# Extra TensorE products whose results nobody reads, ahead of TensorE's waits, and another order of the routing steps

## The chip, the cores and the metric

The kernel runs on one core of a Trainium2 chip. The metric is the device time of one execution in microseconds (us). Five engines work side by side, each through its own instruction queue in program order: PE (TensorE, matrix products; PEld is its weight load), DVE (VectorE), ACT (ScalarE), POOL (GpSimd) and SP (SyncE, which here only starts transfers). They wait for each other through semaphores.

## What is computed

Three blocks with residuals on `x` of 1024 tokens by 512, in float32:

```
x = x + cross_attention(layernorm(x), ctx_768)        # 257 keys of 384 per group of 32 tokens, one head
x = x + self_attention(layernorm(x))                  # 16 heads of 32, rotary, groups of 32 tokens
x = x + experts(layernorm(x))                         # 8 experts, the best 2 of each token

def experts(xf):
    scores = sigmoid(xf @ gate_w.T + balance_bias)    # (tokens, 8)
    top, idx = top_k(scores, 2); top = top / (top.sum() + 1e-6)
    out = sum over the two experts e of a token: top_e * (silu(xf @ w1[e].T) @ w2[e].T)
```

## The kernel before

The 1024 tokens are 8 tiles of 128, worked on in 4 pairs (`PAIRS`). The program of every engine is written out by hand, and its text is the order of its work. There is no scheduler. Matrix products are done in float16 parts (high and low) or in float32, which takes the array several passes.

**Cross attention**, then **self attention** run over the four pairs. In `attend(pair)` PE forms the attention outputs of two tiles (L615), then their output projection: 8 products with the high part (L633) and 4 with the low part (L637) for each tile. ACT and DVE copy and round between them. DVE adds the result to `x` and takes its statistics (`last_stats`, L1464 and L1467), POOL takes the inverse root (L1757), DVE scales (`last_scale`, L1140). PE transposes the scaled rows (`features_T`, L372), ACT copies them (L944) and PE forms the gate's `logits` (L653, products with only 8 columns).

**Routing** is done in three portions, `ROUTED`: tiles 0 to 3, 4 and 5, 6 and 7. For each one DVE ranks the experts (`choose_rank`), PE counts how many tokens chose each expert before this one (`choices_before`, L604), DVE turns counts into places (`place`), marks with one-hot matrices which tokens come first (`mark`, L1567 and L1569), and works out gates (`choose_gates`, L1542 to L1545) and row numbers (`slots_out`, L1575 to L1577). With the row numbers POOL writes every token twice into `routed_rows` in DRAM, sorted by expert: 16 indirect transfers (`scatter`, L1820), two for each tile.

**Experts.** The sorted rows are taken 128 at a time. The first two such tiles need no trip through DRAM: PE gathers their rows by products with the one-hot matrices (`no_rows`, L707, and `first_rows`, L718), ACT copies them into `xgT`. Expert weights come in four pieces; ACT makes each one's high part (`cut_high`, L963) and DVE its low part (`cut_low`, L1614). `first_tile_product` (L751) is the first product of the first tile, then a loop handles the others: `hidden_T` (transposes, L372), `first_product` (L769), `second_product` (L787). ACT's silu is L1065, DVE rounds the hidden rows in `cut_hidden` (L1708 and L1710). POOL adds each finished tile to the output with an indirect transfer (L1856).

What sets the order around the change: PE's text from L628 to L795, DVE's text from L1625 to L1670 and its tail `cut_low(expert0, (1,))`, `tiles_of_experts`, `cut_hidden(0)`, `map_of_tiles`, `cut_low(expert0, (2, 3))`, and the text of ACT behind `features_high(PAIRS - 2)`. Before the change `first_tile_product` begins with two waits:

```
pe.wait_ge(s["rt_slots"], len(ROUTED))
pe.wait_ge(s["xgT0"], 1)
```

`rt_slots` is counted up by the last instruction of each `slots_out`, `xgT0` by ACT's copy of the gathered rows.

## Time and profile before

| | us |
|---|---|
| median of 3 runs (lowest, highest) | 537.12 (536.85, 538.25) |
| the profiled execution's own time | 536.98 |
| its span, first to last instruction | 534.4 |
| PE busy | 490.4 (92% of the span) |
| DVE busy | 374.6 (70%) |
| ACT busy | 254.2 (48%) |
| POOL busy | 111.3 (21%) |
| mean granted share of TensorE's clock | 0.963 |

The share of the clock is given by stretch: 1.00 is 2.4 GHz, 0.50 is 1.2 GHz. The page of the profile cuts the span into 40 slices of 13.4 us; in tenths of busy time and of granted clock they read:

```profile
PE   5998889999999999976879899999999999999994
PEclk9898999999999999986869999999999999999997
```

From the 23rd slice on the expert loop takes over; the slices with gaps in PE's row and a low clock ahead of it (numbers 18 to 22 of the row, 227 to 294 us) are the last pair of self attention, the routing and the first expert tile.

### The profile page before, as it was taken

To read this page: it belongs to the slowest core of one execution; us is meant where nothing else is said; L and a number is where in the kernel's file an instruction comes from. 1 tells how busy PE (TensorE), PEld (TensorE's weight loads), DVE (VectorE), ACT (ScalarE), POOL (GpSimd) and SP (SyncE) were. 2 spreads that over 40 slices of the span, in tenths; PEclk is the share of its full clock that TensorE was granted. 3 is DMA by queue.
4 is the path that set the end of the run, shared out by engine and by line. 5 is a ranking of instruction groups with operands and counts; after the bars stand their busy time and mean duration, and the time that the engine had idled before them with its cause. 6 is when DMAs were issued, how large, how long until landed. Compare 5 with 4: busy or idle time off the path is not lost.

```text
span 534.4 us, 11347 instructions
## 1 busy us (share of the span) xinstructions
PE 490.4 (92%) x3746; PEld 286.0 (54%) x3747; DVE 374.6 (70%) x849; ACT 254.2 (48%) x396; POOL 111.3 (21%) x86
## 2 busy tenths in 40 slices
PE   5998889999999999976879899999999999999994
PEld 2753546555675776735565444445444454444443
DVE  5778898777859998888787886763746637673230
ACT  1313555643359293846732745544625446552230
POOL 1032212012160322200663022111121111121112
PEclk9898999999999999986869999999999999999997
DMA  8999697900009996256842589894885947843333
GB/s 309 405 397 380 242 389 262 371 3 1 1 1 381 379 383 219 72 212 229 288 189 100 154 270 260 270 257 129 230 243 141 258 112 218 238 82 73 59 59 40
DMA packets 55201, 110.95 MB, mean 208 GB/s; under 512 B 24416, under 2 KB 25600, under 8 KB 50048
## 3 DMA queue, kind: packets, MB, share of 16 engines
q1 hardware_dynamic: 25296, 87.80, 45.4%
q10 hardware_dynamic: 25568, 12.94, 10.1%
q0 software_dynamic: 4304, 9.77, 8.6%
q8 instruction: 21, 0.34, 0.3%
q14 instruction: 12, 0.10, 0.1%
HBM read 75.82 MB, written 29.43 MB: 197 GB/s over the span
## 4 chain that ended last, share of the span: by engine, by line
PE 52%; DVE 27%; issue 6%; DMA 5%; ACT 4%; POOL 3%; SPq 2%; DVEq 1%; ACTq 0%; POOLq 0%
PE bank L787 18%; PE bank L769 17%; DMA ctx_region<-in_ctx 4%; PE bank L372 3%; PE bank L540 3%; PE bank L556 3%; DVE wbuf L1614 2%; DVE small L1164 2%; POOL small L1757 2%; DVE small L1161 2%; DVE small L1131 1%; PE bank L751 1%; DVE ctx_region L1411 1%; PE bank L633 1%; DVE ctx_region L1413 1%
## 5 line engine op out<-in xcount | busy, mean ns | idle before, releaser
L769 PE MATMUL bank<-wbuf,ctx_region 128*128 x480 | 106.9, 379 | 0.0
L1614 DVE SCALAR_TENSOR_TENSOR wbuf<-ctx_region,wbuf 128x2048 f32 (+1 forms) x28 | 62.9, 2288 | 29.4 <-ACT wbuf L963 28.0
L1856 POOL DMA_INDIRECT out<-misc,ints x21 | 39.8, 1894 | 203.0 <-ACT misc L1046 144.4
L769 PEld LDWEIGHTS bank<-wbuf,ctx_region 128*128 128x128 f16 x480 | 46.1, 98 | 51.9
L963 ACT ACTIVATE wbuf<-ctx_region 128x2048 f32 (+1 forms) x28 | 52.0, 1902 | 27.6 <-issue 17.2
L1757 POOL TENSOR_TENSOR small<-small 128x2 f32<-128x2 f32 (+2 forms) x25 | 27.4, 1098 | 162.9 <-DVE small L1137 160.1
L1065 ACT ACTIVATE ctxT_region<-bank 128x512 f32<-128x512 f32 x42 | 25.0, 597 | 67.0 <-PE bank L769 56.0
L787 PE MATMUL bank<-wbuf,xn 128*128 x240 | 53.4, 379 | 0.9 <-DVE xn L1714 0.9
L787 PE MATMUL bank<-wbuf,actT 128*128 x240 | 53.4, 379 | 0.0
L787 PEld LDWEIGHTS bank<-wbuf,xn 128*128 128x128 f16 x240 | 23.5, 98 | 29.4 <-issue 1.7
L1708 DVE CAST ctxT_region<-ctxT_region 128x1024 f16<-128x1024 f32 x21 | 14.6, 694 | 34.9 <-ACT ctxT_region L1065 34.9
L787 PEld LDWEIGHTS bank<-wbuf,actT 128*128 128x128 f16 x240 | 23.5, 98 | 28.3
L1710 DVE TENSOR_TENSOR ctxT_region<-ctxT_region 128x1024 f16<-128x1024 f32 x21 | 25.7, 1226 | 0.7
L372 PE MATMUL bank<-ident,ctxT_region 128*128 128x128 f16 x336 | 22.4, 219 | 3.1 <-DVE ctxT_region L1708 1.3
L372 PEld LDWEIGHTS bank<-ident,ctxT_region 128*128 128x128 f16 x336 | 20.4, 98 | 8.4 <-DVE ctxT_region L1708 1.8
L1820 POOL DMA_INDIRECT routed_rows<-shared,ints x16 | 19.1, 1194 | 21.6 <-DVE ints L1577 15.8
L556 PE MATMUL bank<-ctx_region,wbuf 128*128 128x256 f16 x192 | 21.6, 273 | 0.7 <-DVE ctx_region L1288 0.7
L556 PE MATMUL bank<-shared,wbuf 128*128 128x256 f16 x192 | 21.6, 273 | 0.0
L1070 ACT COPY actT<-bank 128x1024 f16<-128x1024 f16 x11 | 11.0, 1001 | 21.9 <-PE bank L372 20.1
L556 PEld LDWEIGHTS bank<-ctx_region,wbuf 128*128 128x128 f16 x192 | 18.7, 98 | 3.5 <-DVE ctx_region L1288 0.9
L1004 ACT ACTIVATE ctxT_region<-ctxT_region 128x512 f32<-128x512 f32 x8 | 5.0, 630 | 32.4 <-DVE ctxT_region L1445 32.4
L986 ACT COPY ctxT_region<-misc 32x512 f32<-32x512 f32 x32 | 19.7, 615 | 1.1 <-DVE misc L1456 0.8
(232 smaller groups left out, 858.9 us busy)
## 6 DMA issues: line engine op xcount, KB each, us to landing
ctx_region<-in_experts SPq DMA_DIRECT2D x28, 1024.0 KB
routed_rows<-ctxT_region SPq DMA_DIRECT2D x1, 16900.0 KB, 50.8
ctxT_region<-in_ctxT SPq DMA_DIRECT2D x8, 1542.0 KB, 11.1
ctx_region<-in_ctx SPq DMA_DIRECT2D x8, 1536.0 KB, 8.9
ctx_region<-routed_rows ACTq DMA_DIRECT2D x21, 260.0 KB, 3.2
wbuf<-in_experts SPq DMA_DIRECT2D x4, 1024.0 KB
out<-x ACTq DMA_DIRECT2D x8, 256.0 KB
wbuf<-in_wqT SPq DMA_DIRECT2D x4, 256.0 KB, 5.3
```

Source lines behind the costliest of these rows:

```text
L372: last = nc.tensor.transpose(dst[0:piece.shape[1], at:at + n], piece, identity[0:n, 0:n])
L556: mm = nc.tensor.matmul(bank[first + e // 2][:, e % 2 * 256:e % 2 * 256 + 256], w[w_part][:, k, e * P:(e + 1) * P], xnT_homes[pair % 2][:, ...
L769: mm = nc.tensor.matmul(bank[half][:, :], xgT[:, b, x_part, k * P:(k + 1) * P], w16[:, ds(at + (w_part + k * EH + half * 512), 512)], star ...
L787: mm = nc.tensor.matmul(bank[5 + b][:, :], hT[b][:, h_part, k * P:(k + 1) * P], w16[:, ds(at + (w_part + W2_AT + k * D), D)], start=(k == ...
L963: nc.scalar.activation(w16[:, ds(at + (HIGH + n * PIECE), PIECE)], src_[:, n * PIECE:(n + 1) * PIECE], ACT.Copy, scale=W_SCALE).then_inc(s ...
L986: op = nc.scalar.copy(p_T[part, t, :, b * L:(b + 1) * L], soft_T[part, t, :].rearrange("p (h l) -> p h l", l=L))
L1065: nc.scalar.activation(h[:, half * 512:half * 512 + 512], bank[half][:, :], ACT.Silu, scale=1.0 / W_SCALE).then_inc(s["h"], 1)
L1614: nc.vector.scalar_tensor_tensor(w16[:, ds(at + (LOW + n * PIECE), PIECE)], src_[:, piece], W_SCALE, w16[:, ds(at + (HIGH + n * PIECE), PI ...
L1710: tt(h16[:, 1, :], h, h16[:, 0, :], ALU.subtract).then_inc(s["h_lo"], 1)
L1757: nc.gpsimd.tensor_tensor(out_, in_, neg_half[0:parts, 0:n], ALU.pow).then_inc(s[f"{name}_rstd"], 1)
L1820: nc.gpsimd.indirect_dma_start(xs_dram, bass.IndirectOffsetOnAxis(slot_i[:, choice, tile:tile + 1].bitcast(U32), axis=0), xf[:, tile, :], ...
L1856: nc.gpsimd.indirect_dma_start(out, bass.IndirectOffsetOnAxis(idx[:, slot_no:slot_no + 1].bitcast(U32), axis=0), y_out[:, slot_no, :], Non ...
```

## The change

1. PE gets a function `unread(b, count)`: `count` products of a 128x128 identity in float16 with itself repeated to 512 columns, written to PSUM bank `b`, where nothing reads them. A new semaphore `ident16_set` tells PE that the identity is there. It is called at nine places, in the order of PE's work with 6, 8, 5, 9, 3, 3, 5, 8 and 4 products (51 in all).
2. The last pair marks tiles 0 and 1 where it marked tiles 0 to 3, and tiles 2 and 3 behind the statistics. PE gathers tiles 2 and 3 behind `features_T(PAIRS - 1)`.
3. `choose_gates(1)` and `slots_out(1)` move behind the marking of the third portion; `cut_low(expert0, (0,))` moves behind `slots_out(2)`.
4. PE gathers tiles 6 and 7 part by part: the high parts of both, then the low parts.
5. `first_tile_product` no longer waits for `rt_slots`; its two halves are now inside the loop over `k`.
6. ACT's `cut_high` of the fourth piece moves behind its copy of the gathered rows.
7. POOL issues 2 of its transfers ahead of the last inverse root, where it issued 3.

```diff
+            def unread(b, count):
+                pe.wait_ge(s["ident16_set"], 1)
+                for _ in range(count):
+                    nc.tensor.matmul(bank[b][:, :], ident16[:, :], ident16[:, None, :].to_broadcast([P, 4, P]), start=True, stop=True,
+                                     skip_group_check=True)
...
                         join_biases()
+                        unread(4, 6)
                         pe.wait_ge(s["sc_nb"], 2)
...
                     pe.wait_ge(s["z"], 2 * pair)
+                if pair + 2 == PAIRS:
+                    unread(0, 8)
+                if pair + 1 == PAIRS:
+                    unread(4, 3)
...
                     scores(pair)
+                    unread(2, 5)
                     features_T(pair - 1)
+                    unread(2, 9)
                     logits(pair - 1)
+                    unread(2, 3)
...
-            first_rows(0, range(0, ROUTED[0][1]))
+            first_rows(0, range(0, 2))
+            unread(6, 5)
             features_T(PAIRS - 1)
+            first_rows(0, range(2, ROUTED[0][1]))
             pe.wait_ge(s["z"], TILES - 2)
             logits(PAIRS - 1)
             first_rows(0, range(*ROUTED[1]))
+            unread(6, 8)
             choices_before(2)
             no_rows(1)
             first_rows(1, range(0, 2))
-            first_rows(0, range(*ROUTED[2]))
+            for part in range(2):
+                first_rows(0, range(*ROUTED[2]), (part,))
...
-                pe.wait_ge(s["rt_slots"], len(ROUTED))
                 pe.wait_ge(s["xgT0"], 1)
...
+            unread(4, 4)
             first_tile_product()
...
-            cut_high(expert0, 2 * EXPERT, (3,), 0)
...
             first_rows_out(0, s["xgT0"], 1)
+            cut_high(expert0, 2 * EXPERT, (3,), 0)
...
-                        mark(0)
+                        mark_at(0)
+                        mark(range(0, 2))
                 norm_mean(stats, mv, ve, s["ln4_ve"], 2)
+                if pair + 1 == PAIRS:
+                    mark(range(2, ROUTED[0][1]))
...
             choose_scores(1)
-            choose_gates(1)
             logits_out(PAIRS - 1)
             choose_rank(2)
-            slots_out(1)
             last_features_low(0)
             place(2)
-            mark(2)
+            mark_at(2)
+            mark(range(*ROUTED[2]))
             last_features_low(1)
-            cut_low(expert0, 2 * EXPERT, (0,), 0)
+            choose_gates(1)
+            slots_out(1)
             choose_experts(2)
             choose_scores(2)
             choose_gates(2)
             slots_out(2)
+            cut_low(expert0, 2 * EXPERT, (0,), 0)
...
-                    scatter(0, first_to_store[0:2])
+                    scatter(0, first_to_store[0:1])
                     features_low(pair - 1)
-                    scatter(0, first_to_store[2:3])
+                    scatter(0, first_to_store[1:2])
```

PE from the last pair's scores to its output projection, before (L592 scores, L372 transposes, L653 logits, L615 attention outputs, L604 counts, L633 projection):

```order
L592 MATMUL bank<-ctx_region 32x128 x32
L372 MATMUL bank<-consts,misc 128x128 x8
L653 MATMUL bank<-gate_w,ctx_region 128x8 x8
L615 MATMUL bank<-ctxT_region,ctx_region 32x128 x16
L604 MATMUL bank<-ctxT_region,late_consts 128x32
L604 MATMUL bank<-ctxT_region,consts 128x32
L615 MATMUL bank<-ctxT_region,ctx_region 32x128 x16
L633 MATMUL bank<-wbuf,actT 128x512 x8
```

The same place in the changed kernel (its line numbers are 8 to 12 higher; L381 is the unread product):

```order
L600 MATMUL bank<-ctx_region 32x128 x32
L381 MATMUL bank<-ident 128x512 x5
L372 MATMUL bank<-consts,misc 128x128 x8
L381 MATMUL bank<-ident 128x512 x9
L665 MATMUL bank<-gate_w,ctx_region 128x8 x8
L381 MATMUL bank<-ident 128x512 x3
L623 MATMUL bank<-ctxT_region,ctx_region 32x128 x16
L612 MATMUL bank<-ctxT_region,late_consts 128x32
L612 MATMUL bank<-ctxT_region,consts 128x32
L623 MATMUL bank<-ctxT_region,ctx_region 32x128 x16
L381 MATMUL bank<-ident 128x512 x3
L645 MATMUL bank<-wbuf,actT 128x512 x8
```

Four groups of unread products have come in, the last of them where no other instruction stood between the attention outputs and the projection. A little later on PE, from the clearing of the gathered rows (L707) to the last counts (L604), before:

```order
L707 MATMUL bank<-ctxT_region 128x512 x2
L718 MATMUL bank<-misc,shared 128x128 x32
L372 MATMUL bank<-consts,misc 128x128 x8
L653 MATMUL bank<-gate_w,ctx_region 128x8 x8
L718 MATMUL bank<-misc,shared 128x128 x16
L604 MATMUL bank<-ctxT_region,late_consts 128x16
L604 MATMUL bank<-ctxT_region,consts 128x16
```

And in the changed kernel (L722 clears, L733 gathers, L665 logits, L612 counts):

```order
L722 MATMUL bank<-ctxT_region 128x512 x2
L733 MATMUL bank<-misc,shared 128x128 x16
L381 MATMUL bank<-ident 128x512 x5
L372 MATMUL bank<-consts,misc 128x128 x8
L733 MATMUL bank<-misc,shared 128x128 x16
L665 MATMUL bank<-gate_w,ctx_region 128x8 x8
L733 MATMUL bank<-misc,shared 128x128 x16
L381 MATMUL bank<-ident 128x512 x8
L612 MATMUL bank<-ctxT_region,late_consts 128x16
L612 MATMUL bank<-ctxT_region,consts 128x16
```

Half of the gathering now stands behind the transposes, and 8 unread products stand ahead of the counts. DVE behind the marking of the third portion (L1569), before (L1486 low part of the features, L1614 the cut of weight piece 0):

```order
L1569 TENSOR_SCALAR misc<-late_consts,small 128x256 x2
L1486 TENSOR_TENSOR shared<-misc,shared 128x512
L1614 SCALAR_TENSOR_TENSOR wbuf<-wbuf 128x2048
L1522 TENSOR_SCALAR ctxT_region<-ctxT_region 128x16
L1523 TENSOR_SCALAR ctxT_region<-ctxT_region 128x16
```

And in the changed kernel (L1590 marks, L1505 low part, L1561 to L1564 gates of the second portion, L1596 to L1598 its row numbers, L1541 the third portion's experts):

```order
L1590 TENSOR_SCALAR misc<-late_consts,small 128x256 x2
L1505 TENSOR_TENSOR shared<-misc,shared 128x512
L1561 SCALAR_TENSOR_TENSOR ctxT_region<-ctxT_region 128x2
L1563 RECIPROCAL ctxT_region<-ctxT_region 128x2
L1564 SCALAR_TENSOR_TENSOR shared<-ctxT_region 128x2x2
L1596 TENSOR_TENSOR ctxT_region<-ctxT_region,misc 128x2x16
L1597 TENSOR_REDUCE misc<-ctxT_region 128x2x2
L1598 CAST ints<-misc 128x2x2
L1541 TENSOR_SCALAR ctxT_region<-ctxT_region 128x16
```

Six small instructions have taken the place of the cut of piece 0; that cut now stands directly ahead of the cut of piece 1, behind the row numbers of the third portion.

## Rows read from the trace of the kernel before

**Rows 1.** Chain that ended last, in order of time: start us, us, what.

```profile
230.94 2.62 PE bank L633 x8
...
238.06 0.70 DVE x L1464
...
279.70 7.05 PE bank L751 x24
...
317.45 5.18 PE bank L769 x24
```

**Rows 2.** PE's waits from 225 to 312 us: line <- releaser: total, times, longest.

```profile
PE bank L372 <- DVE misc L1140: 3.6, 2, 1.8
PE bank L653 <- ACT ctx_region L944: 3.4, 2, 3.1
PE bank L751 <- DVE ints L1577: 3.1, 1, 3.1
PE bank L633 <- DVE small L1493: 2.8, 1, 2.8
```

**Rows 3.** Stretches: us, busy us (x) of each engine, granted clock third from last.

```profile
242.80:245.50 2.70, 0.00 (x0) 0.00 (x0) 2.63 (x5) 1.46 (x3) 0.00 (x0) 1.00 0.37 100
245.70:255.70 10.00, 9.70 (x88) 7.75 (x89) 8.04 (x29) 7.89 (x19) 0.49 (x1) 0.50 0.64 220
266.20:276.20 10.00, 9.96 (x67) 9.14 (x68) 8.46 (x31) 4.82 (x7) 6.33 (x7) 0.50 0.58 218
279.90:283.00 3.10, 3.10 (x8) 1.06 (x7) 2.96 (x9) 0.00 (x0) 2.27 (x2) 0.50 0.08 30
```

**Rows 4.** Timeline of PE and DVE around 50 us: start, us, instruction [idle before].

```profile
47.20 5.40 PE L445 MATMUL bank<-wbuf 128*128 128x512 f32 x8 [2.29 <-DVE small L1232]
...
53.12 0.68 DVE L1352 SCALAR_TENSOR_TENSOR bo<-rows,bo 32x512 f16<-32x512 f32 x1
53.83 0.42 DVE L1251 TENSOR_TENSOR misc<-bank,small 128x256 f32<-128x256 f32 x1
```

**Rows 5.** Timeline of PE, 219 to 263 us.

```profile
219.18 5.34 PE L582 MATMUL bank<-wbuf,shared 128*128 128x512 f16 x24
224.36 1.85 PE L653 MATMUL bank<-gate_w,ctx_region 128*128 128x8 f32 x16
...
245.83 3.58 PE L653 MATMUL bank<-gate_w,ctx_region 128*128 128x8 f32 x16 [3.08 <-ACT ctx_region L944]
...
252.44 1.94 PE L615 MATMUL bank<-ctxT_region,ctx_region 128*32 128x128 f32 x32
...
261.03 1.95 PE L718 MATMUL bank<-misc,shared 128*128 128x128 f16 x32
```

**Rows 6.** Timeline of DVE, 252 to 298 us.

```profile
252.54 0.77 DVE L1559 TENSOR_TENSOR misc<-bank,misc 128x8 f32<-128x8 f32 x4 [0.98 <-PE bank L604]
...
259.18 0.86 DVE L1567 SCALAR_TENSOR_TENSOR small<-ctxT_region,misc 128x4 f32<-128x4 f32 x1
...
261.31 0.67 DVE L1464 SCALAR_TENSOR_TENSOR x<-bank,x 128x512 f32<-128x512 f32 x1
...
273.93 0.68 DVE L1486 TENSOR_TENSOR shared<-misc,shared 128x512 f16<-128x512 f32 x1
274.54 2.28 DVE L1614 SCALAR_TENSOR_TENSOR wbuf<-wbuf 128x2048 f16<-128x2048 f32 x1
...
287.41 0.69 DVE L1708 CAST ctxT_region<-ctxT_region 128x1024 f16<-128x1024 f32 x1 [3.09 <-ACT ctxT_region L1065]
...
296.08 4.49 DVE L1614 SCALAR_TENSOR_TENSOR wbuf<-ctx_region,wbuf 128x2048 f16<-128x2048 f32 x2
```

**Rows 7.** Timeline of POOL, 272 to 287 us.

```profile
275.75 1.90 POOL L1820 DMA_INDIRECT routed_rows<-shared,ints  x1 [0.31 <-issue]
...
280.43 2.24 POOL L1820 DMA_INDIRECT routed_rows<-shared,ints  x1 [1.51 <-DVE ints L1577]
...
285.75 0.96 POOL L1820 DMA_INDIRECT routed_rows<-shared,ints  x1 [0.30 <-issue]
```

More of the change, by code:

```diff
@@ L85 @@
 qk_ps qkT qb_ps q_bias sc_ps max_step sc_nb sc_exp sc_rinv sc_pm pT_ps pT cv_ps cv_raw cv cvT_ps y_ps x_new
-ptx_zero ln3_ve ln3_rstd ln3_out xnT_ps xnT xnT_lo sw_hi sw_lo sq_ps sk_ps sq sk swapped cosined sined
+ident16_set ptx_zero ln3_ve ln3_rstd ln3_out xnT_ps xnT xnT_lo sw_hi sw_lo sq_ps sk_ps sq sk swapped cosined sined
 rotated k_exp sv_ps sv ss_ps softmax_step s_sub s_exp s_pT p_cols ao_ps ao_hi ao_lo sy_ps x_post x_plus_sbo
@@ L708, in no_rows, with first_rows @@
                                      skip_group_check=True)
-            def first_rows(n, tiles):
+            def first_rows(n, tiles, parts=(0, 1)):
                 for tile in tiles:
                     pe.wait_ge(s["hot"], tile + 1)
-                    pe.wait_ge(s["xf_lo"], tile + 1)
-                    for part in range(2):
+                    for part in parts:
+                        pe.wait_ge((s["xf_hi"], s["xf_lo"])[part], tile + 1)
                         for k in range(KC):
@@ L720, in first_rows @@
                                                   start=False, stop=(tile == TILES - 1), skip_group_check=True)
-                if tile == TILES - 1:
+                if tile == TILES - 1 and 1 in parts:
                     mm.then_inc(s["xgT_ps"], 1)
@@ L734, in _ @@
             first_rows(1, range(0, 2))
-            first_rows(0, range(*ROUTED[2]))
+            for part in range(2):
+                first_rows(0, range(*ROUTED[2]), (part,))
             def first_tile_product():
                 at = 2 * EXPERT
-                pe.wait_ge(s["rt_slots"], len(ROUTED))
                 pe.wait_ge(s["xgT0"], 1)
                 for w_part, x_parts in ((HIGH, (0, 1)), (LOW, (0,))):
-                    for half in range(2):
-                        for k in range(KC):
-                            if w_part == LOW:
-                                pe.wait_ge(s["w1_lo"], k // 2 + 1)
-                            else:
-                                pe.wait_ge(s["w_hi"], k // 2 + 1)
+                    for k in range(KC):
+                        pe.wait_ge(s["w1_lo"] if w_part == LOW else s["w_hi"], k // 2 + 1)
+                        for half in range(2):
                             for x_part in x_parts:
@@ L753, in first_tile_product @@
                                                       stop=(k == KC - 1 and w_part == LOW), skip_group_check=True)
-                        if w_part == LOW:
-                            mm.then_inc(s["h_ps"], 1)
+                            if w_part == LOW and k == KC - 1:
+                                mm.then_inc(s["h_ps"], 1)
             def experts_of(tile):
@@ L1305, in _ @@
                                     ALU.add)
-            nc.vector.tensor_copy(ident16[:, :], ident)
+            nc.vector.tensor_copy(ident16[:, :], ident).then_inc(s["ident16_set"], 1)
             dve.wait_ge(s["cols_in"], 16)
@@ L1560, in place, with mark_at, mark @@
                 then(tt(slot[:, some], bank[within][:, lo * E:hi * E].rearrange("p (t e) -> p t e", e=E), base[:, some, :], ALU.add))
-            def mark(n):
-                lo, hi = ROUTED[n]
-                some = slice(lo, hi)
+            def mark_at(n):
+                some = slice(*ROUTED[n])
                 dve.wait_ge(s["rt_sel"], n + 1)
                 then(nc.vector.scalar_tensor_tensor(hot_at[:, some], sel[:, some, 0], -CHOSEN, slot[:, some, 0], ALU.mult, ALU.add))
-                for tile in range(lo, hi):
+            def mark(tiles):
+                for tile in tiles:
                     ts(hot[:, tile, :], late("places"), hot_at[:, tile:tile + 1], None, ALU.is_equal).then_inc(s["hot"], 1)
@@ L1670, in _ @@
             place(1)
-            mark(1)
+            mark_at(1)
+            mark(range(*ROUTED[1]))
             choose_experts(1)
             choose_scores(1)
-            choose_gates(1)
             logits_out(PAIRS - 1)
             choose_rank(2)
-            slots_out(1)
             last_features_low(0)
             place(2)
-            mark(2)
+            mark_at(2)
+            mark(range(*ROUTED[2]))
             last_features_low(1)
-            cut_low(expert0, 2 * EXPERT, (0,), 0)
+            choose_gates(1)
+            slots_out(1)
             choose_experts(2)
@@ L1843, in _ @@
                     plus_sbo(pair + 2)
-            scatter(0, first_to_store[3:])
+            scatter(0, first_to_store[2:])
             for n in (1, 2):
```

## The prediction

> **What bounds the kernel now.** I read the chain that ended last first. From 317.45 us on it holds PE alone, product after product [rows 1], and no step of the change lies there. So the change is worth what the loop starts earlier. Ahead of it the chain passes between PE and DVE in 228 to 311 us. PE's waits name four gaps there, of 2.8 to 3.6 us in total per line [rows 2]. The stretches then show what follows such gaps: the granted clock is still 1.00 at 242.80 to 245.50, where PE has nothing, and 0.50 (1.2 GHz) in the 10 us behind it, though PE is busy for 9.70 us of them; the same in 266.20 to 276.20 and behind the wait for L751 in 279.90 to 283.00 [rows 3].
>
> At 0.50 the logits (L653) take 3.58 us against 1.85 at 1.00, and 32 records of L615 take 1.94 [rows 5], about half of that (0.98) at 1.00. On 32 gathering products (L718, 1.95 us at 1.00, so 0.98 for 16) it is the same doubling. An unread product has the shape of L582, 24 in 5.34 us [rows 5]: 0.22 us each at 1.00, 0.43 at 0.50.
>
> **Ahead of L445 (6 products).** 6 x 0.22 = 1.3 us in a wait of 2.29 us [rows 4], so it costs nothing. If the clock holds, L445 takes some 3.7 instead of 5.40 us, but DVE comes to L1251, which waits for the transposes behind it, straight from L1352 (53.80 to 53.83) [rows 4]. DVE is full there: 0 gained.
>
> **Pair 2's projection (8 products).** 1.7 us in the wait of 2.8 us [rows 2]. The 24 projection products behind it would take 5.3 us at 1.00 where they took 7 from 230.94 [rows 1]. DVE's choice of experts stands between its two additions, so the second one, L1464 at 238.06 [rows 1], comes when DVE is free: 1.06 earlier. The scores, the softmax and its copies on ACT follow. Lead: 1.06.
>
> **The last pair (5, 9, 3 and 3).** The first 5 and 9 take 1.1 and 1.9 us of waits of about 1.8 and 3.08 us and delay nothing. But will they hold the clock? Behind the 9 there is still about 1.2 us of nothing, then the logits, 3, and 1.2 us more until the softmax's copies come. With the logits as full-time work the clock stayed at 0.50 in 245.70 to 249 [rows 3, 5], so they do not bring it up. I judge it likelier that it falls once more, and take the attention outputs at 0.50. Then the count for DVE's L1559 is there at 251.5 rather than 252.54 (lead 1.04 [rows 6]), the second half ends at 253.45, and the 3 products in front of the projection, which stood in no wait, cost 3 x 0.43 = 1.3 us. The projection's second tile ends near 260.55, where it ended just before 260.4. DVE's second L1464 was held at 261.31 not by PE but by the marks. Two marks fewer (0.65) and L1567, which took 0.86 us beside POOL's subtraction [rows 6] and now comes after it, make DVE free, so PE's 260.6 decides. Lead at the scaled rows: 0.7.
>
> That L1567 waited is what the Trainium skill, "SBUF — State Buffer", section "Who interferes with whom", says of a DVE instruction with two SBUF inputs and a GpSimd one that reads SBUF: one fully blocks for the other. It returns as a rival below.
>
> **Transposes, logits, counts.** The projection has brought the clock up by then, and 5 products and the gathering keep work dense. Transposes 264.05 to 265.1, gathering of tiles 2 and 3 to 266.1 (0.98, moved behind them; ACT's copy needs most of that), logits 1.85 to 267.95. They ended at 269.7, so the lead is 1.75. DVE has its ranks at 269.7. PE gathers tiles 4 and 5 to 268.9 and then stands in 8 unread products until 270.65, 0.95 after the ranks: that is the price of this group. Counts to 271.2, which came at 272.5: lead 1.3. DVE's marks and last low part, L1486 at 273.93 with 0.68 [rows 6], end at 273.2: lead 1.4.
>
> **The reordered tail on DVE.** Before, DVE went on with the cut of piece 0 (2.28), 3 us of small instructions, the cut of piece 1, the tile tables (2.55), and then stood 3.09 us at L1708 for ACT's silu, since PE had stood for the row numbers until 279.70 [rows 1, 2, 6]. Now 1.2 us of gates and row numbers of portion two come first. PE gathers to 274, ACT copies to 275, PE does the 16 high products (3.5 us) meanwhile, and the 8 low ones follow the two cuts, which end at 281.7; the silu is done by 283.7, and DVE comes to L1708 at 284.25 without a wait, 3.15 us before 287.41. The 4 products in front cost nothing, since ACT's copy takes as long. On its own DVE would have the first cut of the loop's weights at 293.0 instead of 296.08 [rows 6].
>
> **POOL.** Row numbers of portion two are now at 274.4 (before: 271.9), so 8 of the 16 transfers stand behind them. Free of cuts one takes 0.96 with 0.30 in front [rows 7], 1.26. Issued during a cut it took 1.90 and 2.24, each ending 0.9 us after that cut did [rows 6, 7]. From 275.3, with cuts in 277.3 to 281.7: 276.3, 278.0, 280.4, 282.6, then 4 x 1.26: 287.65. It ended at 286.71 before, so this queue is later than before by 0.94 and becomes what is late next. ACT waits for its last write (about 1.4 us to land), reads rows, copies the hidden tile, and makes the high part that DVE's cut needs: 6.1 us from POOL's end, 293.75. That is a lead of 2.3 us over 296.08. The first inverse root has one transfer fewer ahead of it, but POOL was free 2 us before it was asked: 0.
>
> **PE in front of the loop.** PE now finishes its second product at about 298 and waits 3 us for the rounded rows, where it waited 1.3. Behind waits of that size the clock fell [rows 2, 3]. Half a fall (3.4 us at 0.50 lose 1.7 in 279.90 to 283.00 [rows 3]) is hidden under DVE's copy, 0.9 us late for PE before. So between 0 and 0.8 us are lost; I take 0.4.
>
> **Sum:** 536.98 - 2.3 + 0.4 = 535.1 for a profiled execution (its span of 534.4 and 2.6 around it). The median of the runs stood 0.14 above that execution: 535.2.
>
> **Costs with two ends.** Each unread product lies between 0.22 and 0.43 us, by the clock it meets. The early group: 0 to 1.3 us if sc_nb came first, which the 2.29 us exclude. The 8 in front of the counts: 0.95 us, or 2.6 at 0.50.  A transfer of POOL during two joined cuts: 1.26 to 4 us; I take the single cut's figures, the nearest rows.
>
> **Rivals.**
>
> 1. *The clock holds through the last pair.* For it: 14 dense products in two waits, and the clock did stay at 1.00 behind the 1.8 us wait at 240. Then the attention outputs end at 252.0, the 3 products cost nothing more than 0.65, the projection ends at 257.85, DVE's L1464 comes at 257.9, logits end at 265.6, counts at 268.8 (8 products overshoot by 0.85), the last low part at 270.6: lead 4.0. The tail adds what it adds above (2.3 less 1.4, 0.9): the first loop cut at 291.2, lead 4.9, less 0.4, plus 0.14: 532.6.
>
> 2. *No change: POOL is shut out by the joined cuts.* A transfer that meets the first cut waits for the second too, ends at 282.6 instead of 280.4, and five follow: 288.9, 1.25 later. With the full 0.8 at the loop: 536.98 - 2.3 + 1.25 + 0.8 + 0.14 = 536.9. Against it: POOL got its turn within 0.9 us of a cut's end both times. For it: nothing stands between the cuts now. By the page of the Trainium skill named above, whichever of the two engines is first holds the pair for its whole instruction, and a cut has two SBUF inputs; if DVE's second cut is first each time, that rule gives this case's time.
>
> 3. *Slower: the 8 products in front of the counts meet a clock of 0.50.* The logits alone kept it there before [rows 3], and gathering tiles 2 and 3 late leaves gaps around the transposes. Logits then end at 270.5, gathering at 272.4, the 8 take 3.46 us instead of 1.73, counts at 276.9, 4.4 us late. As dense work they may bring the clock up halfway, which gives back 1.7. The tail takes 0.9 off: 1.8 to 3.5 late, middle 2.6: 536.98 + 2.6 + 0.14 = 539.7. It turns to a loss once the counts are later than 273.4 (272.5 and the 0.9 that the tail still gives).
>
> **Chances.** Forecast 0.41, rival 1 0.27, rival 2 0.18, rival 3 0.14. What a measurement can tell from no change is about 0.3%, 1.6 us: faster means under 535.5, slower over 538.7. The forecast's own range is 534.0 to 536.3, about 0.65 of it under 535.5. Faster: 0.27 + 0.27 = 0.54; slower 0.14; within 0.32. The range reaches to rival 1 and to the near end of rival 3: 532.2 to 538.2.
>
> **What would show it.** Right: the clock at 1.00 from 228 to about 246, at 0.50 for part of 246 to 256, at 1.00 through 264 to 270; L751's row with two short waits for DVE's cuts in place of one of 3.1 us for row numbers; no wait at DVE's L1708; POOL's 16th transfer ending near 287.7; the loop's first cut near 293.8. Rival 1 shows the clock at 1.00 throughout and that cut near 291. Rival 2 shows a POOL transfer of over 3 us. Rival 3 shows the clock at 0.50 over the 8 products and counts behind 273. I am wrong altogether if the loop's products show gaps behind 320 us that they did not have.

## The result, and the profile after

| | median, us (lowest to highest, runs) | ratio to the kernel before, 95% interval |
|---|---|---|
| first set: the changed kernel | 541.07 (537.71 to 541.84, 6) | 1.0059 [1.0032, 1.0086] |
| the kernel before beside it | 536.99 (535.41 to 538.56, 6) | |
| second set, taken later: the changed kernel again | 536.85 (536.05 to 538.83, 12) | 0.9984 [0.9966, 1.0001] |
| the kernel before beside it | 537.59 (534.41 to 539.55, 32) | |

Slower in the first set, no difference in the second. The forecast was 535.2, likelier faster than not. Neither set bears it out. Two executions far from all others (999.68 us of the kernel before beside the first experiments, 730.26 us of c_order_only) are in no ratio. The rows below are of the profiled execution of the first set: 541.43 us, span 539.5, mean granted clock 0.977 (before: 0.963).

The chain that ended last (start, us, what) answers to [rows 1]. The lines have other numbers in the changed kernel: L645 was L633, L1480 was L1464, L766 was L751 and L784 was L769; L1635 (DVE's cut of expert weights) was L1614 and L1843 (GpSimd's transfers) was L1820. The four rows now read:

```profile
237.69 1.73 PE bank L645 x8
...
242.96 0.70 DVE x L1480
...
309.75 6.78 PE bank L784 x24
...
322.60 5.18 PE bank L784 x24
```

The expert loop's product from which PE works without gaps (the steady product below) stands 5.15 us later than in [rows 1] (322.60 for 317.45), and DVE's second addition already 4.90 later (242.96 for 238.06). So the loss in this execution lies ahead of everything in the tail. The stretches (columns as in [rows 3]) show where the clock now is and is not:

```profile
57.00:63.00 6.00, 6.00 (x32) 1.50 (x25) 5.93 (x14) 1.17 (x5) 0.69 (x1) 0.50 0.49 172
98.00:101.00 3.00, 3.00 (x8) 0.84 (x7) 2.04 (x9) 2.37 (x5) 0.00 (x0) 0.50 0.99 413
247.70:250.40 2.70, 1.88 (x9) 0.68 (x7) 2.63 (x5) 1.46 (x3) 0.00 (x0) 1.00 0.44 112
255.00:258.00 3.00, 3.00 (x48) 2.49 (x42) 2.03 (x10) 2.94 (x8) 0.00 (x0) 0.50 0.80 317
271.10:281.10 10.00, 8.31 (x77) 5.33 (x77) 6.71 (x31) 3.69 (x6) 3.86 (x5) 1.00 0.44 165
306.20:312.60 6.40, 4.91 (x24) 2.70 (x25) 4.61 (x6) 3.93 (x4) 1.62 (x1) 0.50 0.75 239
```

Of the 0.50 stretches of [rows 3] one part is left, 255 to 258; 271 to 281 is at 1.00 throughout. New ones are at 57, 98 and 306. The unread products keep the clock up there: c_order_only below, the same order without them, has it at 0.50 in 233.4 to 236.8, 247.1 to 257.3 and 270.9 to 277.8 us (one trace each). But it didn't pay. The last expected step of the tail is there too. DVE's and GpSimd's timeline around it, to be read against [rows 6, 7]:

```profile
282.37 4.49 DVE L1635 SCALAR_TENSOR_TENSOR wbuf<-wbuf 128x2048 f16<-128x2048 f32 x2
289.25 0.69 DVE L1731 CAST ctxT_region<-ctxT_region 128x1024 f16<-128x1024 f32 x1
300.26 2.29 DVE L1635 SCALAR_TENSOR_TENSOR wbuf<-ctx_region,wbuf 128x2048 f16<-128x2048 f32 x1 [2.26 <-ACT wbuf L979]
```

```profile
274.26 0.96 POOL L1843 DMA_INDIRECT routed_rows<-shared,ints  x1 [0.30 <-issue]
280.45 0.96 POOL L1843 DMA_INDIRECT routed_rows<-shared,ints  x1 [5.23 <-DVE ints L1598]
...
282.98 2.50 POOL L1843 DMA_INDIRECT routed_rows<-shared,ints  x1 [0.30 <-DVE ints L1598]
285.79 1.90 POOL L1843 DMA_INDIRECT routed_rows<-shared,ints  x1 [0.31 <-issue]
...
292.33 0.96 POOL L1843 DMA_INDIRECT routed_rows<-shared,ints  x1 [0.30 <-issue]
```

The two cuts of weight pieces 0 and 1 now follow each other at once, L1731 (L1708 before) has lost its wait of 3.09 us, and the loop's first cut has got one of 2.26: GpSimd sat idle for 5.23 us for the row numbers of the second portion (tiles 4 and 5; portion 1 in the code and below), its last transfer ends at 293.29, and what ACT does for that cut comes behind it. Last, PE's waits from 230 to 317 us, against [rows 2]:

```profile
PE bank L372 <- DVE ctxT_region L1731: 3.5, 1, 3.5
PE bank L381 <- issue: 2.8, 1, 2.8
PE bank L766 <- DVE wbuf L1635: 2.0, 2, 1.2
```

L381 is the unread product. The wait of 2.8 us of pair 2's projection is now charged to it: the product stands behind that wait in PE's program and does not fill it.

### The profile page after: what moved, and what is told of

Its sections match the earlier page's. It is cut to its first block, busy times and chain, and to the rows that moved or that the text cites. A ratio compares the mean times of both kernels' runs of the same rounds, so it can differ in the third digit from the quotient of the medians.

```text
span 539.5 us, 11451 instructions
## 1 busy us (share of the span) xinstructions
PE 495.7 (92%) x3797; PEld 284.1 (53%) x3798; DVE 373.9 (69%) x849; ACT 254.2 (47%) x396; POOL 110.8 (21%) x86
## 4 chain that ended last, share of the span: by engine, by line
PE 59%; DVE 18%; issue 7%; DMA 7%; POOL 4%; ACT 2%; SPq 2%; ACTq 0%; DVEq 0%; POOLq 0%
PE bank L784 19%; PE bank L802 18%; DMA ctx_region<-in_ctx 6%; PE bank L372 4%; PE bank L564 4%; PE bank L548 3%; POOL routed_rows L1843 2%; DVE small L1180 1%; PE bank L529 1%; POOL small L1780 1%; DVE small L1147 1%; DVE small L1177 1%; PE bank L828 1%; PE bank L590 1%; PE bank L645 1%
## 5 line engine op out<-in xcount | busy, mean ns | idle before, releaser
L784 PE MATMUL bank<-wbuf,ctx_region 128*128 x480 | 108.5, 383 | 0.0
L1635 DVE SCALAR_TENSOR_TENSOR wbuf<-ctx_region,wbuf 128x2048 f32 (+1 forms) x28 | 62.9, 2289 | 32.9 <-ACT wbuf L979 31.5
L784 PEld LDWEIGHTS bank<-wbuf,ctx_region 128*128 128x128 f16 x480 | 46.6, 99 | 53.1 <-issue 2.2
L1731 DVE CAST ctxT_region<-ctxT_region 128x1024 f16<-128x1024 f32 x21 | 14.6, 693 | 31.6 <-ACT ctxT_region L1081 31.5
L372 PE MATMUL bank<-ident,ctxT_region 128*128 128x128 f16 x336 | 23.2, 223 | 5.0 <-DVE ctxT_region L1731 3.5
L372 PEld LDWEIGHTS bank<-ident,ctxT_region 128*128 128x128 f16 x336 | 21.0, 100 | 10.4 <-DVE ctxT_region L1731 4.0
L1843 POOL DMA_INDIRECT routed_rows<-shared,ints x16 | 19.0, 1189 | 23.2 <-DVE ints L1598 19.5
```

The lines of the kernel that those rows point to most:

```text
L372: last = nc.tensor.transpose(dst[0:piece.shape[1], at:at + n], piece, identity[0:n, 0:n])
L784: mm = nc.tensor.matmul(bank[half][:, :], xgT[:, b, x_part, k * P:(k + 1) * P], w16[:, ds(at + (w_part + k * EH + half * 512), 512)], star ...
L1635: nc.vector.scalar_tensor_tensor(w16[:, ds(at + (LOW + n * PIECE), PIECE)], src_[:, piece], W_SCALE, w16[:, ds(at + (HIGH + n * PIECE), PI ...
L1843: nc.gpsimd.indirect_dma_start(xs_dram, bass.IndirectOffsetOnAxis(slot_i[:, choice, tile:tile + 1].bitcast(U32), axis=0), xf[:, tile, :], ...
```

## The experiments

All ratios are to the kernel before on the same chip. The traces are compared at fixed instructions: the start in the kernel's trace less the start in the trace before, each less the same shift at 220.65 us (the turning of pair 2's features), so that what happened ahead of the tail is taken out. Negative is earlier. The columns are named by the line and time in the kernel before: L1464, DVE's second addition of pair 2's projection; the last low part of the features (L1486); L1708, DVE's first rounding of hidden rows; DVE's first cut of weights in the expert loop (L1614); PE's steady product (L769). Worked out so:

| kernel | ratio | shift at 220.65 | L1464 at 238.06 | last low part, 273.93 | L1708, 287.41 | first loop cut, 296.08 | steady product, 317.29 |
|---|---|---|---|---|---|---|---|
| changed, first set | 1.0059 | +4.91 | 0.0 | -1.0 | -3.1 | -0.7 | +0.2 |
| changed, second set | 0.9984 | +3.03 | +1.7 | -1.5 | -3.6 | -1.6 | -0.5 |
| a_no_early | 1.0041 | +1.02 | +1.7 | +1.1 | -1.0 | +1.0 | +1.0 |
| b_only_early | 1.0006 | +1.71 | -1.2 | -2.1 | -2.5 | -2.5 | -2.5 |
| c_order_only | 1.0027 | +1.71 | -0.1 | +0.7 | -1.4 | +0.5 | +2.0 |
| d_products_only | 1.0065 | +0.80 | +1.7 | +1.8 | +0.1 | +0.2 | +0.2 |
| e_slots_early | 0.9942 | +2.56 | +1.7 | -1.2 | -4.4 | -4.4 | -3.8 |
| f_ahead_of_wait | 0.9961 | +0.85 | -1.2 | -4.5 | -6.5 | -4.6 | -3.5 |
| g_logits_first | 1.0033 | +4.83 | +1.7 | +1.6 | -0.5 | +1.7 | +2.3 |
| i_both | 0.9955 | +0.84 | -1.2 | -1.6 | -4.8 | -4.8 | -4.8 |
| j_both_hold | 0.9934 | +2.48 | -1.2 | +0.5 | -2.7 | -2.7 | -2.0 |
| k_both_four | 0.9921 | +2.17 | -1.2 | -0.6 | -3.8 | -3.8 | -3.8 |
| l_both_without_three | 0.9950 | +0.40 | -1.2 | -0.1 | -3.3 | -3.3 | -3.3 |
| m_logits_first_none | 1.0020 | +2.84 | -1.3 | +3.6 | +0.6 | +0.7 | +0.7 |
| n_without_early | 0.9958 | +1.23 | -1.2 | -1.5 | -4.7 | -4.7 | -4.7 |
| o_without_unread_tail | 0.9978 | +1.03 | -1.2 | -0.8 | -3.8 | -3.8 | -3.2 |
| p_both_four_again | 0.9971 | +1.10 | -1.2 | +1.4 | -1.8 | -1.8 | -1.8 |

One trace each, while the ratios rest on 6 to 12 runs. The two need not agree: d_products_only's trace is 1.0 us late at the steady product, its ratio says 3.5 us.

### Which half of the change costs

```diff
# a_no_early (the changed kernel without this line)
-                        unread(4, 6)
# b_only_early (the kernel before with this line ahead of L445)
+                        unread(4, 6)
# c_order_only: the changed kernel without any unread(...)
# d_products_only: the kernel before with every unread(...) but the early one
```

> The changed kernel without the six unread products ahead of L453. Theory A (they are the cause): with them the profile of the changed kernel had granted clock 1.00 at 47.6 to 51.0 us and 0.50 at 56.9 to 63.6, where the context products stand in the chain, and pair 2's L623 ended 4.9 us late (233.00 for 228.10). Without them the 0.50 comes back at 47.6 to 51.0, L623 ends near 228.1 to 229, and the time is 541.1 - 4.9 + up to 1 = 536 to 537.5, the same as before. Theory B (the 4.9 us are a chance of landing times, and the loss lies elsewhere, as in the products behind the wait in pair 2's projection): L623 lands anywhere from 228 to 233, and the time stays at 540 to 542.

> The kernel before with only the six unread products ahead of L445. Theory A: clock 1.00 at 47 to 51 us and 0.50 soon after 56 us; pair 2's L615 ends 3 to 5 us later than 228.1, and the time is 537.0 + 3 to 5 = 540 to 542, a loss as large as the whole change's. Theory B: no difference beyond 0.3%, 535.5 to 538.5, wherever the clock falls.

> The changed kernel without any of the unread products: the other order alone. Theory A: nothing is lost upstream (L615 of pair 2 ends 228 to 229), and in the tail the order gives nothing, since GpSimd's sixteen scatters end near 288 to 290 as in the changed kernel and hold ScalarE's weight conversions; 536 to 538. Theory B, for which the order is what costs (gates and slots of portion 1 later, so scatters later): the first loop cut is later than 296.08 and the time is 538 to 542.

> The order before with the unread products of the last three stages, without the six early ones. Theory A: L615 of pair 2 ends 228 to 229; the 8 products of pair 2's projection stand behind the wait of 2.8 us and cost 1.7, the warm clock afterwards gives back 1 to 2; the wait at L1708 stays and moves with its place; 536 to 538. Theory B (the products cost what they take wherever TensorE is late): 3 products 0.65, 8 products 1.7, 5 of them in a row about 1, not repaid: 539 to 541.

Measured: 1.0041 [1.0013, 1.0069], 1.0006 [0.9981, 1.0031], 1.0027 [1.0, 1.0054], 1.0065 [1.0029, 1.01]. Theory A, on which the six early products bring the loss, falls: alone they cost nothing, and without them the loss stays. The products of the tail lose by themselves. Of the order alone the interval just reaches 1. In the table five traces lose 1.7 us at the second addition of pair 2: a, d, e, g and the second of the changed kernel, all with the 8 products behind the wait. PE's timeline of d, with the products alone, says why:

```profile
231.68 2.48 PE L381 MATMUL bank<-ident 128*128 128x512 f16 x8 [2.79 <-issue]
233.95 3.03 PE L644 MATMUL bank<-wbuf,actT 128*128 128x512 f16 x8
```

PE waits 2.79 us, and only then come the 8 products, with the projection behind them.

### The two suspected places, one at a time

```diff
# e_slots_early: DVE's order
             choose_scores(1)
+            choose_gates(1)
             logits_out(PAIRS - 1)
             choose_rank(2)
+            slots_out(1)
             last_features_low(0)
...
-            choose_gates(1)
-            slots_out(1)
# f_ahead_of_wait: in attend
                 elif pair + 1 < PAIRS:
+                    if pair + 2 == PAIRS:
+                        unread(1, 8)
                     pe.wait_ge(s["z"], 2 * pair)
-                if pair + 2 == PAIRS:
-                    unread(0, 8)
# g_logits_first: after features_T(PAIRS - 1)
-            first_rows(0, range(2, ROUTED[0][1]))
             pe.wait_ge(s["z"], TILES - 2)
             logits(PAIRS - 1)
+            first_rows(0, range(2, ROUTED[0][1]))
# h_changed_again: the changed kernel as it is
```

> The changed kernel with portion 1's gates and slots back at their place ahead of the last pair's low features. Theory T (GpSimd's scatters are what the tail waits for): the idle stretch of 5.2 us ahead of GpSimd's seventh scatter goes, its sixteenth ends at 288 to 289 instead of 293.3 (both less the drift of the stages before), the first loop cut no longer waits 2.3 us for ScalarE, and the kernel is 1.5 to 2.5 us faster than the changed kernel on this chip. Rival (TensorE's own wait and the clock in front of the loop set the end): the first loop cut comes earlier, the steady loop does not, and the time moves by less than 0.5 us.

> The changed kernel with pair 2's 8 unread products ahead of the wait for the choice's logits instead of behind it (in bank 1, which is free there). Theory T: they now lie in the idle time of 2.8 us and cost nothing, so DVE's L1480 of pair 2 is earlier by 1.7 us, and so is the end: 1.2 to 1.7 us faster than the changed kernel. Rival (whatever is late at that projection, something else is next, a few tenths later): less than 0.5 us.

> The changed kernel with the last pair's logits issued ahead of the 16 row products of tiles 2 and 3 instead of behind them. In the changed kernel DVE waits 1.2 and 0.5 us for these logits, and in the one with the order alone 1.2 and 1.9; in the kernel before 0 and 0.8. Theory T (the row products in front delay the logits, by more than their records show): both waits together fall below 1 us, the last rank is 0.8 to 1.2 us earlier. Part of it reaches the end only if GpSimd's scatters do not set it: 0 to 1 us faster than the changed kernel. Rival (the lateness of the logits comes from TensorE's clock or from the transposes): the waits stay at 1.7 to 3 us and nothing moves.

> The changed kernel itself, so that the three others are compared with it on one chip. If the 0.50 stretches at 56.9 to 63.6 and at 97.9 to 101.2 come from the six early products, they are here again and pair 2's L623 ends 3 us or more late; if they were a chance of one run, they are not, and L623 ends 0.5 to 1.8 us late, as in the four kernels of the first set. The time by the first: 540 to 542; by the second 539 to 540.5.

Measured: 0.9942 [0.9916, 0.9968], 0.9961 [0.9942, 0.998], 1.0033 [1.0006, 1.0059], 0.9984 [0.9966, 1.0001]. Both mends are worth what was expected: by the ratios 0.42% (2.3 us) and 0.23% (1.2 us) against the changed kernel, by the medians beside each other 1.8 and 1.9 us (535.02 and 534.94 for 536.85). Nearly every run of e lies below the changed kernel's fastest (532.89 to 536.09 for 536.05 to 538.83); f reaches further in (533.73 to 537.06). The products ahead of the wait, PE's timeline of f_ahead_of_wait:

```profile
228.87 1.90 PE L381 MATMUL bank<-ident 128*128 128x512 f16 x8
231.74 1.90 PE L645 MATMUL bank<-wbuf,actT 128*128 128x512 f16 x8 [0.97 <-DVE small L1512]
```

The same 8 products now leave 0.97 us of the wait, and the projection runs at 1.00. In the table this place has three values: +1.7 (products behind the wait and the clock falls all the same), 0 or -0.1 (behind the wait and the clock holds, or no products and it falls) and -1.2 (the clock holds and nothing stands in the way). The eight later kernels with this mend all show -1.2 or -1.3.

With portion 1's row numbers early, GpSimd's and DVE's timeline of e_slots_early:

```profile
273.01 0.96 POOL L1843 DMA_INDIRECT routed_rows<-shared,ints  x1 [0.30 <-issue]
274.28 0.96 POOL L1843 DMA_INDIRECT routed_rows<-shared,ints  x1 [0.31 <-issue]
```

```profile
294.22 4.49 DVE L1635 SCALAR_TENSOR_TENSOR wbuf<-ctx_region,wbuf 128x2048 f16<-128x2048 f32 x2
```

GpSimd goes on without its 5 us of idle, and the first loop cut has no wait. In the table the lead at L1708 reaches the first loop cut undiminished in every kernel with this mend; without it 1.9 to 2.4 us are given back (the changed order in a, c, f, g and both traces of the changed kernel).

g_logits_first did the reverse of what was expected: the logits came at once (no wait), but DVE then stood 3.11 us for the counts, for which 32 row products and the 8 unread ones were now in front. It is slower than the changed kernel, by 2.9 us in the medians (539.72 for 536.85).

h_changed_again: the 0.50 stretches at 57 and 98 did not come again. A fall that begins at 56 to 59 us is in the traces of g, i, n and p too, of which n has no early products, and in none of the others; the one at 98 came only once. So they are not what the change brings each time. Two traces, the changed kernel's and f_ahead_of_wait's, have every start of DVE, ACT and GpSimd up to 57 us within 0.2 us of each other (half of DVE's from 30 us on within 0.01), and only the first has the fall there. The same stretches of the second:

```profile
57.00:63.00 6.00, 4.70 (x46) 2.28 (x39) 5.93 (x14) 2.89 (x9) 0.69 (x1) 1.00 0.61 224
98.00:101.00 3.00, 3.00 (x20) 2.04 (x18) 2.17 (x6) 1.48 (x3) 0.00 (x0) 1.00 1.04 437
```

### Both mends, and what is left to try

```diff
# i_both: e and f together.  j_both_hold: i, and in context_sums
                     tile = 2 * pair + t
+                    if tile == 0:
+                        unread(2, 5)
# k_both_four: i with
-            unread(6, 8)
+            unread(6, 4)
# l_both_without_three: i without
-                if pair + 1 == PAIRS:
-                    unread(4, 3)
```

> The changed kernel with both mends: pair 2's 8 unread products ahead of the wait, and portion 1's gates and slots at their earlier place. Apart they measured 0.9961 and 0.9942 of the time before, the changed kernel 0.9984 beside them. Theory T (two different waits, one behind the other on the same path): the two gains add, 0.9984 - 0.0023 - 0.0042 = 0.992, some 533 us. Rival (both end at the same next wait, TensorE's in front of the second tile's product): no better than the better of the two, 0.994 to 0.996.

> The same with five more unread products ahead of the first context sums, in a wait of 1.3 us. Theory T (the spread between executions comes from whether the clock falls to 0.50 at 57 to 66 us, where the context sums stand in the chain): with the wait filled the clock stays at 1.00 there, no execution loses the 2 to 4 us, and both the median and the spread fall: spread (highest less lowest) below 4 us for 5 to 9 in earlier kernels, median 0 to 1 us lower. Rival (the clock falls elsewhere, or the landing times make the spread): the spread stays at 4 us or more, and the median is the same or 0.3 higher.

> As the first kernel of this set, with 4 unread products ahead of the last counts instead of 8. In the changed kernel on this chip's twin DVE waited 0.72 us for the counts because TensorE was still at the 8. Theory T (this wait is on the path to the rows of the first tile): it goes, and the kernel is 0.4 to 0.7 us faster than with 8. Rival (the clock then falls at the following products, or GpSimd's scatters hide it): within 0.3 us or slower.

> As the first kernel of this set without the three unread products ahead of the last pair's projection. Theory T (TensorE is late there, so they cost what they take, 0.65 us, and the clock holds without them): 0.4 to 0.7 us faster. Rival (they keep the clock up, which the last pair's projection needs): the clock falls at 247 to 258 us for two or three stretches instead of one, and the kernel is 0.5 to 1.5 us slower.

Measured: 0.9955 [0.993, 0.9979], 0.9934 [0.9911, 0.9958], 0.9921 [0.9893, 0.9949], 0.995 [0.9923, 0.9977], medians 535.2, 534.68, 533.9 and 534.54 us. All four beat the kernel before (the changed kernel was not run beside them), and their intervals overlap: no order among them is shown. i_both's ratio is in the range of its rival (0.994 to 0.996) and did not reach the 0.992 of added gains, though its trace has the largest lead of all at the steady product (-4.8): whether the two gains add is open. j's spread is 4.6 us for i's 5.5, both above the 4 expected: filling that one wait is not the cure.

### The late logits

```diff
# m_logits_first_none: k with g's order, and without
-            unread(6, 4)
# n_without_early: k without unread(4, 6)
# o_without_unread_tail: k without unread(6, 4)
# p_both_four_again: k as it is
```

> The kernel with both mends and 4 products ahead of the last counts, changed in two places: the last pair's logits ahead of the row products of tiles 2 and 3, and no unread products ahead of the counts, since the 32 row products now fill that wait. In 7 of 9 traces with the changed order of these two, TensorE's last logits reached DVE 1.6 to 3.0 us after TensorE's records of them end; in the 3 with the order before and the 1 with logits first, 0 to 0.7. Theory T (the 16 row products in front bring that lateness): it is gone here, and the kernel is 1 to 2 us faster than the one with four products. Rival (it comes and goes between executions): still there in this trace or in the median, no faster.

> The kernel with both mends and four products, without the six early unread products ahead of L453. If they bring the fall of the clock at 57 to 66 us that cost the first profile of the changed kernel 3 to 4 us, it is faster or its spread is smaller: 0.5 to 1.5 us. If that fall comes by chance with or without them, the same within 0.3%. If they hold off a fall at 42 to 51 us that costs, it is slower by up to 0.5 us.

> The kernel with both mends, and no unread products at all ahead of the last counts (8 in the changed kernel, 4 in the best so far). Eight cost 0.72 us as a wait of DVE in the changed kernel. If four are free and hold the clock for the counts and row products behind them, this one is 0.5 to 1 us slower than with four; if they only take TensorE's time, the same or up to 0.4 us faster.

> The best kernel so far once more, beside the three others on their chip: 0.9921 of the time before in the last set, by which 0.990 to 0.995 here. The lateness of the last logits (3.0 us in its first trace) comes again if the order of row products and logits brings it; a trace without it would say that it comes and goes.

Measured: 1.002 [0.9998, 1.0043], 0.9958 [0.9936, 0.998], 0.9978 [0.9958, 0.9999], 0.9971 [0.9947, 0.9995]. The six early products are worth nothing that can be measured, and 0, 4 or 8 ahead of the counts can't be told apart. m loses 3.4 us against p in the medians (538.86 for 535.49), where a gain of 1 to 2 us was expected; it differs from p in two places, but o, without the four products as well, does not lose so, which leaves the order.

What it looks like, first in f_ahead_of_wait and then in i_both: PE's logits, and DVE's two additions that take them.

```profile
264.07 1.90 PE L665 MATMUL bank<-gate_w,ctx_region 128*128 128x8 f32 x16
265.70 0.47 DVE L1512 TENSOR_TENSOR small<-bank,rows 128x8 f32<-128x8 f32 x2
```

```profile
264.03 1.90 PE L665 MATMUL bank<-gate_w,ctx_region 128*128 128x8 f32 x16
266.89 0.17 DVE L1512 TENSOR_TENSOR small<-bank,rows 128x8 f32<-128x8 f32 x1 [0.66 <-PE bank L665]
268.95 0.17 DVE L1512 TENSOR_TENSOR small<-bank,rows 128x8 f32<-128x8 f32 x1 [1.89 <-remote]
```

PE's records are alike within 0.04 us and the granted clock is 1.00 in both, yet DVE gets the second logits at 266 in one and 268.9 in the other. "Remote" means that no record accounts for the release: PE's ends are modelled, and here the second logits were released 3.0 us later than they say. In m, with the logits first, it is the row products behind them that drag. PE's timeline, then DVE's:

```profile
273.07 0.28 PE L733 MATMUL bank<-misc,shared 128*128 128x128 f16 x2 [0.49 <-issue]
273.79 0.23 PE L733 MATMUL bank<-misc,shared 128*128 128x128 f16 x1 [0.43 <-issue]
274.52 0.34 PE L733 MATMUL bank<-misc,shared 128*128 128x128 f16 x3 [0.50 <-issue]
275.94 0.59 PE L733 MATMUL bank<-misc,shared 128*128 128x128 f16 x4 [1.08 <-issue]
```

```profile
279.00 0.37 DVE L1577 TENSOR_TENSOR misc<-bank,misc 128x8 f32<-128x8 f32 x2 [7.26 <-remote]
```

Sixteen such products take 1.05 us elsewhere; here they stutter for nearly 7 us, and DVE gets the counts that stand ahead of them in the queue 7.1 us behind the end of their records (271.89). The granted clock in this trace is 0.50 in 268.5 to 271.9 and again from 275.3 us, but 1.00 where the first gaps are. Of the 13 traces with row products directly ahead of the logits, 10 have the lateness, 1.6 to 4.5 us; the three without it (h, e, f) come from one chip, on which no trace has it; g's, with the logits first, is from that chip too and says nothing. Of the other traces with another order there, before, b and d are free of it, and m has it one step later. On one chip the order alone told them apart (a and c have it, b and d don't, one trace each); that the chip also decides is not excluded. So the sluggish stretch goes with row products at 264 to 279 us, and the new order puts something that DVE waits for behind them. What slows PE there is open; no run separated GpSimd's transfers, which run at the same time, from it.

The version with both mends and four products ahead of the counts measured 0.9921 [0.9893, 0.9949] and 0.9971 [0.9947, 0.9995] in two sets; both intervals lie below 1.

## Why the prediction was wrong, point by point

**Ahead of L445: right.** Nothing gained, nothing lost (b: 1.0006; n against p).

**Pair 2's projection: the step whose mechanism failed.** "1.7 us in the wait of 2.8 us": the wait stands ahead of `unread`, in program order, so the products came behind it and cost their 1.7 us. The gain of the clock was sized well (1.06; every trace with the clock up and nothing in the way has 1.2). Instead of a lead of 1.06 it was 0.0 in the first set and -1.7 in the second. f showed it by moving the call ahead of the wait: -1.2, and 1.9 us in the medians.

**The last pair: right in kind, better than forecast.** The clock fell once more, in 255 to 258 only. Between the second addition (table, 238.06) and the scaled rows the first trace gained 1.5 us where the step has the lead shrink from 1.06 to 0.7. That this makes good what pair 2 had missed, a lead of 1.5 at the scaled rows for 0.7 forecast, is luck: two errors against each other.

**Transposes, logits, counts: the overshoot was right, the logits were not foreseen.** DVE waited 0.82 us for the counts in the first trace and 0.72 in the second, forecast 0.95. But the second logits were 1.6 us late in the first trace, and up to 4.5 in later kernels, for which no row stood in the profile before.

**DVE's tail: right.** No wait at L1708, 3.1 us earlier than before against its own start (forecast 3.15).

**GpSimd as what is late next: right in kind, undersized, and with the next term what the forecast of the tail failed by.** Less the 4.9 us its last transfer ended at 288.4 (forecast 287.65, 0.74 off). The cut came 6.97 us behind it for 6.1: the last write landed 2.2 us behind the end of its instruction, not 1.4 (no row has 1.4; in the profile before, too, the last landing seen is 1.8 us behind, at 288.49). Together the cut was 1.6 us later than forecast, a lead of 0.7 instead of 2.3. Rival 2's form, a transfer shut out by both cuts, did not happen: the first transfer at the pair ended 285.48, 0.8 us behind the first cut (282.37 + 2.28), the next 0.8 behind the second. The Trainium skill, "SBUF — State Buffer", section "Who interferes with whom", says that a DVE instruction with two SBUF inputs contends with a GpSimd one that reads SBUF. The trace agrees (2.50 and 1.90 us for 0.96). The Trainium skill says in the same section, of DVE's two-port modes, that whichever engine issues first holds the ports for its whole instruction; that DVE's second cut would come first, as rival 2 had it, no trace here shows.

**In front of the loop: undersized.** PE waited 3.5 us (forecast 3), and the clock fell for the whole of 306 to 313: 0.96 us in the first trace, 1.08 in the second, for 0.4.

The three last terms account for the tail: -1.9 forecast, + 0.74 + 0.87 + 0.56 = +0.3, measured +0.2. In the first trace, then, the end is missed by GpSimd's last transfer, the way from it to the cut and PE in front of the loop; e, with GpSimd's row numbers early, ends the tail at -3.8.

The larger part of the first trace's miss lies ahead of the tail, in stages for which the prediction had no term. The execution took 541.43 us for 535.1 forecast: 4.9 us ahead of the tail and 2.1 in it, less 0.7 because the time around the span was 1.9 us for 2.6. Of the 4.9, 0.85 come from a transfer of context rows that DVE waits for at 33 us (all sixteen later traces are 0.4 to 3.0 us late behind it), 1.6 us from the clock's fall at 98, and 2.5 us in one wait at 89 us, where the granted clock is 1.00: DVE stands for the landing of context rows. DVE and SyncE's issue of that transfer, in the first trace and then in f's:

```profile
90.87 1.94 DVE L1177 BATCH_NORM_STATS2 small<-ctx_region 128x6 f32<-128x384 f32 x4 [1.94 <-DMA ctx_region<-in_ctx]
81.57 2.64 SPq L296 DMA_DIRECT2D ctx_region<-in_ctx  x2
```

```profile
88.35 1.94 DVE L1177 BATCH_NORM_STATS2 small<-ctx_region 128x6 f32<-128x384 f32 x4
81.56 2.64 SPq L296 DMA_DIRECT2D ctx_region<-in_ctx  x2
```

PE had made good the fall at 57 by then (L524 starts at 79.18 and 79.17 us). g has the same fall and the same wait and is 2.4 us later behind it; n and p have the fall and lose 0.75 and 0.5. So whether the fall brings the late landing is open, and so is why the other five executions of the first set, which left no trace, took 537.71 to 541.84 us at a mean clock of 0.976 to 0.982. The second set's 536.85 us lies in the forecast's range, but not for its reasons: its tail was ahead by 0.5 us for 1.9.

I had taken one execution's clock for the kernel's. Over the 32 runs of the kernel before beside the first experiments, those with mean clock 0.972 took 534.1 to 535.7 us and those with 0.963 took 536.3 to 540.8. So how often the clock falls goes with the time in one and the same program, and a forecast of 1.8 us out of one trace's falls stands on little. Rival 1 and rival 3 are out: the clock did not hold throughout, and it was at 1.00 over the 8 products ahead of the counts.

## What to carry to other kernels

Filler work hides in a wait only if it is issued ahead of the instruction that waits; look at the program order of the wait, not at the gap in the timeline. When an order is changed to take away one wait, follow each result that is now produced later to the queue that is slowest to use it (here row numbers, behind which 8 of GpSimd's 16 transfers stand, 1.3 us each). And before counting on the clock, see in how many executions it falls there.

## What the runs showed of the hardware

- The granted clock of one program falls at different places from run to run: with the starts of three engines within 0.2 us of each other up to 57 us, one execution had 0.50 in 57 to 63 us and the other 1.00.
- PE's records of the second logits end 1.6 to 4.5 us before DVE gets them, in 10 traces of 13 with many 128x128 f16 products around them, with the granted clock at 1.00 over the logits; in m's trace 16 such products took nearly 7 us with gaps of 0.3 to 1.1 us for which the profile has no cause.
- Two context transfers issued at the same time (81.57 and 81.56 us) in two executions: in one DVE had to wait for the rows until 90.87 us, in the other it read them at 88.35 without a wait.
- A GpSimd indirect transfer that meets a DVE cut of 2.28 us ends 0.8 us behind it, and gets its turn between two cuts that follow at once (2.50 and 1.90 us for 0.96).
